# Last node stage of a four-layer graph network: TensorE turns the rows of a block two blocks, instead of one, before it multiplies them

## The chip, the cores and the metric

One Trainium2 chip, one of its cores. The metric is the device time of one execution in microseconds. The kernel has four layers; the change is in the second half of the last one.

## The reference

Four graph layers run one after the other on 50,000 nodes with 160 features (64 scalars and 32 vectors of three) and 25,000 edges. Each layer computes, cut to what matters here:

```python
agg = segment_sum(edge_feat, edge_dst)            # edge stage: messages summed per target node
# node stage of the last layer (L3), for every node:
s_s = xs * node_attr @ Ws_sc_a + xs * node_crystal_attr @ Ws_sc_c     # 64 scalars, two groups of weights
s_v = same with the 32 vectors and Wv_sc_a, Wv_sc_c
out = C_S * concat(s_s, s_v) + C_X * o            # o: made from agg
x   = _layernorm(x + out)                         # over the 160 features
```

So the node stage reads each node's row x and its aggregate row, adds the two, adds two products of x with small matrices, each scaled by one of the node's two gates, and normalises the row.

## The kernel before

Each layer l (0 to 3) has an edge stage, which writes the aggregates to memory, and then a node stage. A node stage goes over `NBLK` = 100 blocks b of 512 nodes; a block lies as 128 partitions with `BT` = 4 rows of 160 features each (`xn[:, k]`, 640 columns). Eight slots, `NRING` = 8, k = b % 8, hold the blocks in flight. The engines' programs are written out by hand, one instruction stream for each, with semaphores between them; on every engine the order is fixed, and a wait holds up all that stands behind it. In the last layer (l = 3, `G` = 2 groups of weights) the streams are, for step b:

- SyncE's queue, `node_loads`: wait for `stored[k]`, that is until the result of block b - 8 has left the slot; then load x of block b (line 476), and then the aggregates of block b + 2 (line 465).
- TensorE, `node_products`: the turn of block b (line 816: five 128x128 transposes, written T(b) below), once x of block b is in (`x_in`) and the PSUM pair `two_banks[b % 2]` is free, that is once ScalarE has copied turn b - 2 (`nturned_out`). Then the products of block b - 1 (line 846: eight fp32 matmuls that the trace shows as sixteen records, P(b-1) below). P(b) waits for the copy of turn b, for VectorE to be done with the first half of P(b-1) (`y_stt`; PSUM banks 4 and 5), and in its middle for ScalarE to be done with the second half (`second_gated`; banks 6 and 7).
- ScalarE, `node_copies`: issue the store of block b - 5 (line 959, from `STORE_LAG` = 5); copy turn b from PSUM to `nT[b % 2]` (line 963), once T(b) and P(b-2) are done; scale the second half of the products of block b - 1 into `second` (line 974, four instructions), once P(b-1) is done; the square root for block b - 3 (line 980); the normalisation of block b - 4 (line 986, four instructions).
- VectorE, `node_vectors`: add the first half of P(b), scaled, to the rows (line 1300, four instructions); then the statistics of block b - 1 (lines 1317 and 1328), and between them the reciprocal and the shift for block b - 2 (lines 1277 and 1282), which wait for ScalarE's square root.
- GpSimd, `add_both`: add the aggregates of block b to x once T(b) has read it (line 645), then the two scaled halves of block b - 1 (lines 651 and 654).

`steps` writes the first eight steps out, runs steps 8 to 95 as a loop with eight steps in its body, and writes the last ones out. `back(k, turn, lag, ring)` gives the slot and the turn of an earlier block, and `within(q, lo, hi)` says whether step q has work of that kind. The program waits that matter:

```python
wait(pe, nturned_out, node_count(l, b - 2))          # line 813, ahead of T(b)
wait(act, sc_ready, 2 * (b + (l * NBLK - 1)))        # line 962, ahead of the copy of turn b
act.wait_ge(sc_ready, 2 * (b + l * NBLK))            # line 970, ahead of the scaling of block b - 1
wait(sp, stored[k], node_slot(l, k, turn - 1) * 16)  # line 474, ahead of the load of x
```

Of the kernel before, what the change touches and what calls it, by code (L numbers as in the profile page):

```python
# [24 lines left out]
NBLK = 100  # L25
# [8 lines left out]
APPLY_LAG = [4, 3, 3, 4]  # L34
STORE_LAG = [5, 4, 4, 5]
A_LEAD = 2
NRING = 8
XGR = 4
AW = 2 + F
# [101 lines left out]
def back(k, turn, lag, ring=RING):  # L141

    return (k - lag) % ring, turn + (k - lag) // ring


def steps(eng, first, last, steady, body, ring=RING):

    lo, hi = steady
    for q in range(first, lo):
        body(q, q % ring, q // ring)  # L150
    with eng.Fori(0, (hi - lo) // ring) as i:
        for k in range(ring):
            body(i * ring + (lo + k), k, i + lo // ring)
    for q in range(hi, last):
        body(q, q % ring, q // ring)


def within(q, lo, hi):

    return lo <= q < hi if isinstance(q, int) else True  # L160


def wait(eng, sem, value):

    if isinstance(value, int) and value <= 0:
        return
    eng.wait_ge(sem, value)


def alone(eng, passed):  # L170

    eng.sem_inc(passed, 1)


def build(nc, nodes, front, back_rows, gate_rows, pairs, eattr, main, small, self_rows, mark_rows, out):
# [3 lines left out]
    with ctx:  # L179
        def sb(name, shape, dt=f32):  # L180
            return ctx.enter_context(nc.sbuf_tensor(name, shape, dt))

        def sem(name):
            return ctx.enter_context(nc.semaphore(name))
# [44 lines left out]

        arena = sb("arena", [P, NRING * BT * (F + AW)])  # L230
        o1, o2, o3, o4 = 512, 512 + 4 * 384, 512 + 4 * 384 + 4 * F, 1536 + 4 * 384 + 4 * F
# [4 lines left out]
        tot = arena[:, o4:o4 + TRING * 2 * (2 + AW3)].rearrange("p (r t c) -> p r t c", r=TRING, t=2)  # L236
        n1 = NRING * BT * F
        n2 = n1 + NRING * BT * AW
        xn = arena[:, 0:n1].rearrange("p (r c) -> p r c", r=NRING)
        an = arena[:, n1:n2].rearrange("p (r t c) -> p r t c", r=NRING, t=BT)  # L240
        second = same_all[:, 0:XGR * BT * F].rearrange("p (r t c) -> p r t c", r=XGR, t=BT)
        attr = sb("attr", [P, NRING, BT, 3])
        stats = sb("stats", [P, 2, BT, 6])
# [88 lines left out]
        nturned, nturned_out, sc_ready = sem("nturned"), sem("nturned_out"), sem("sc_ready")  # L332
# [6 lines left out]
        gated, second_gated, second_added = sem("gated"), sem("second_gated"), sem("second_added")  # L339
# [7 lines left out]
        NODE_STEADY = (NRING, 96)  # L347
# [13 lines left out]
        def node_count(l, b):  # L361
            return b + (l * NBLK + 1)
# [3 lines left out]
        def node_slot(l, k, turn):  # L366

            return turn + (l * node_uses[k] + 1)
# [18 lines left out]
        def _(sp):  # L387
# [26 lines left out]
            for l in range(4):  # L414
# [43 lines left out]
                def aggregate_load(b, k):  # L458
                    at = b if isinstance(b, int) else sp.snap(b)
                    if l in (0, 3):  # L460
                        wait(sp, x_added, b + ({0: 1, 3: NBLK + 1}[l] - NRING) if not isinstance(b, int) or b >= NRING else 0)
                    elif not isinstance(b, int) or b >= NRING:
                        wait(sp, sc_ready, 2 * (b + (l * NBLK + 1 - NRING)))
                    alone(sp, passed["sp"])
                    sp.dma_start(an[:, k].rearrange("p t c -> p (t c)"),
                                 arows[bass.ds(at, 1)].rearrange("o p c -> (o p) c")).then_inc(a_in[k], 16)

                def node_loads(b, k, turn):
                    if isinstance(b, int) and b == 0:
                        for n in range(A_LEAD):  # L470
                            aggregate_load(n, n)
# [4 lines left out]
                    sp.dma_start(xn[:, k], xrows[bass.ds(at, 1)].rearrange("o p c -> (o p) c")).then_inc(x_in[k], 16)  # L476
                    if within(b, 0, NBLK - A_LEAD):
                        aggregate_load(b + A_LEAD, (k + A_LEAD) % NRING)

# [190 lines left out]
        def _(pe):  # L670
# [26 lines left out]
            for j in range(4):  # L697
                a, b = (384, 448) if j < 2 else (448, 480)
# [7 lines left out]
            for l in range(4):  # L706
# [98 lines left out]

                def node_products(b, k, turn):

                    kk, tt = back(k, turn, 1, NRING)
                    has_new, has_old = within(b, 0, NBLK), within(b, 1, NBLK + 1)
                    if has_new:  # L810
                        to = two_banks[k % 2]
                        pe.wait_ge(x_in[k], node_slot(l, k, turn) * 16)
                        wait(pe, nturned_out, node_count(l, b - 2))
                        alone(pe, passed["pe"])
                        for c in range(5):
                            last = nc.tensor.transpose(to[:, c * P:(c + 1) * P], xn[:, k, c * CH:(c + 1) * CH], ident[:, :])  # L816
                        last.then_inc(nturned, 1)
                    if not has_old:
                        return
                    pe.wait_ge(nturned_out, node_count(l, b - 1))  # L820
                    base = 2 * (b + l * NBLK)
                    turned_x = [nT[:, kk % 2, c * P:(c + 1) * P] for c in range(5)]
                    mm = nc.tensor.matmul
                    if G == 1:
                        A, B = bank[4 + 2 * (kk % 2)], bank[5 + 2 * (kk % 2)]
                        wait(pe, y_stt, base - 4)
                        alone(pe, passed["pe"])
                        fresh = l == 0
                        if not fresh:
                            pe.wait_ge(a_in[kk], node_slot(l, kk, tt) * 16)  # L830
                            alone(pe, passed["pe"])
                            mm(A[:, 0:3 * F].rearrange("p (t c) -> p t c", t=3), ident[:, :], an[:, kk, 0:3, 2:AW], start=True, stop=False)
                        for c in range(4):
                            o, e = c * CH, min((c + 1) * CH, 3 * F)
                            last = mm(A[:, o:e], turned_x[c], sc[l][:, o:e], start=fresh, stop=fresh or c == 3)  # L835
                        last.then_inc(sc_ready, 1)
                        if not fresh:
                            mm(B[:, 0:F], ident[:, :], an[:, kk, 3, 2:AW], start=True, stop=False)
                        mm(B[:, 0:F], turned_x[4], sc[l][:, 3 * F + S:4 * F + S], start=fresh, stop=False)
                        mm(B[:, 0:S], turned_x[3], sc[l][:, 3 * F:3 * F + S], start=False, stop=True).then_inc(sc_ready, 1)  # L840
                    else:
                        two = lambda ap, n: ap.rearrange("p (g c) -> p g c", c=n)
                        W = two(sc[l], SCC)

                        def product(j, lo, hi, c, at, **flags):
                            return mm(two(bank[4 + j][:, 0:2 * F], F)[:, :, lo:hi], turned_x[c], W[:, :, at:at + hi - lo], **flags)  # L846
                        whole = dict(start=True, stop=True)
                        wait(pe, y_stt, base - 2)
                        alone(pe, passed["pe"])
                        product(0, 0, 128, 0, 0, **whole)  # L850
                        product(0, 128, 160, 1, 128, **whole)
                        product(1, 0, 96, 1, 160, **whole)
                        product(1, 96, 160, 2, 256, **whole).then_inc(sc_ready, 1)
                        wait(pe, second_gated, b - 1)
                        alone(pe, passed["pe"])
                        product(2, 0, 64, 2, 320, **whole)
                        product(2, 64, 160, 3, 384, **whole)
                        product(3, 0, 160, 4, 544, start=True, stop=False)
                        product(3, 0, 64, 3, 480, start=False, stop=True).then_inc(sc_ready, 1)

                steps(pe, 0, NBLK + 1, NODE_STEADY, node_products, NRING)

                pe.wait_ge(y_stt, 2 * NBLK * (l + 1))

# [555 lines left out]
```

## Time and profile before

| what | value |
|---|---|
| median of three runs | 4107.62 us (4105.41 to 4110.64) |
| profiled execution, its own time | 4101.09 us |
| span of the profiled execution | 4098.9 us |
| mean granted TensorE clock over the span | 0.949 |
| busy share of the span: TensorE, VectorE, ScalarE, GpSimd | 86%, 68%, 55%, 61% |
| last node stage: first turn of TensorE, last copy of turned rows on ScalarE | 3644.50 us, 4081.6 us |

The busy shares are means over stages with different limits. A span lies inside the execution's own time, and 2.2 us are outside it. Line numbers with L are those of the kernel. In the trace PE is TensorE's matmuls, PEld its weight loads, DVE VectorE, ACT ScalarE, POOL GpSimd; ACTq and SPq are instructions of the sequencers, the issues of transfers among them. An idle time is put down to what came last by the profile, which need not be what the program waited for.

### The profile page before, as it was taken

The numbers are of one execution on the slowest core, as the hardware profiler recorded it, in microseconds if no ns is written. First come the engines' busy times: TensorE is split into PE (matmuls) and PEld (weight loads), VectorE is DVE, ScalarE is ACT, GpSimd is POOL, SyncE is SP. The second block draws the span as 40 slices with busy tenths as digits, with TensorE's granted clock in tenths as the row PEclk, the third lists the DMA queues.
The fourth block names the chain that finished last, engine by engine and source line by source line (L and its number), as shares of the span: only waits on it lengthen the run. The fifth ranks groups of instructions, "written<-read, shape, count | busy, mean of one in ns | idle before, by whom it ended". The sixth has DMA issues, their size and how long they took to land.

```text
span 4098.9 us, 104392 instructions
## 1 busy us (share of the span) xinstructions
PE 3520.8 (86%) x26652; PEld 3264.2 (80%) x26652; DVE 2803.2 (68%) x10450; ACT 2255.1 (55%) x6189; POOL 2500.3 (61%) x3168
## 2 busy tenths in 40 slices
PE   0599998666659999989979999989989999977776
PEld 0599997656649999977769999977779999976665
DVE  0477775888876666668876666678866666656666
ACT  0244443555544444457765555567766666658888
POOL 0377776777766777756657777600036666657776
PEclk9999999777769999999999999999999999989999
DMA  9522222556642222259862222178842222136665
GB/s 390 179 82 63 61 56 86 187 196 200 202 137 59 58 57 55 48 192 300 298 200 64 62 61 57 39 271 300 298 130 56 54 52 50 44 109 223 222 226 193
DMA packets 423009, 575.44 MB, mean 140 GB/s; under 512 B 218250, under 2 KB 241802, under 8 KB 419144
## 3 DMA queue, kind: packets, MB, share of 16 engines
q1 hardware_dynamic: 280746, 293.10, 24.3%
q10 hardware_dynamic: 60512, 166.57, 10.3%
q0 software_dynamic: 81648, 114.57, 9.8%
q8 instruction: 43, 0.70, 0.1%
q14 instruction: 60, 0.49, 0.0%
HBM read 359.42 MB, written 233.39 MB: 145 GB/s over the span
## 4 chain that ended last, share of the span: by engine, by line
PE 60%; ACT 15%; POOL 8%; issue 8%; ACTq 3%; DMA 2%; DVE 2%; another core or an unknown queue 2%; POOLq 1%; SPq 1%; DVEq 0%
PE bank L734 17%; PE bank L767 12%; ACT arena L986 9%; PE bank L777 5%; PE bank L787 3%; PE bank L724 3%; PE bank L790 3%; PE bank L741 3%; PE bank L782 3%; POOL arena L632 3%; ACT same_all L974 3%; PE bank L759 3%; ACTq L959 2%; POOL arena L636 2%; ACT nT L963 2%
## 5 line engine op out<-in xcount | busy, mean ns | idle before, releaser
L545 POOL DMA_INDIRECT aggregates<-arena,meta x784 | 792.0, 1010 | 436.5 <-issue 252.5
L986 ACT ACTIVATE arena<-arena,shift,rstd 128x160 f32<-128x160 f32 x1600 | 699.3, 514 | 180.3 <-DVE shift L1251 177.6
L734 PE MATMUL bank<-same_all,msg 128*98 (+1 forms) x6272 | 750.7, 273 | 0.0
L533 POOL DMA_INDIRECT xg<-x_after,meta x588 | 584.7, 994 | 252.7 <-issue 249.7
L734 PEld LDWEIGHTS bank<-same_all,msg 128*98 128x98 f32 x6272 | 708.0, 165 | 0.1
L903 ACT ACTIVATE w<-bank 1x162 f32<-1x162 f32 (+1 forms) x784 | 257.9, 329 | 738.2 <-PE bank L767 736.5
L767 PE MATMUL bank<-w,arena 98*128 98x32 f32 (+1 forms) x4704 | 626.8, 270 | 0.0
L835 PEld LDWEIGHTS bank<-sc_cols,nT 128*128 128x128 f32 x2400 | 358.8, 220 | 288.7 <-issue 287.3
L767 PEld LDWEIGHTS bank<-w,arena 98*128 98x128 f32 x4704 | 588.6, 192 | 0.0
L835 PE MATMUL bank<-sc_cols,nT 128*128 128x128 f32 (+1 forms) x2400 | 371.3, 306 | 178.0 <-ACT nT L963 157.6
L1317 DVE BATCH_NORM_STATS2 stats<-arena 128x6 f32<-128x160 f32 x1600 | 455.5, 314 | 42.2 <-DVE arena L1310 5.8
L963 ACT ACTIVATE nT<-bank 128x640 f32<-128x640 f32 x400 | 281.6, 705 | 331.0 <-PE bank L835 165.0
L1206 DVE TENSOR_TENSOR arena<-bank,yv 128x192 f32<-128x192 f32 x294 | 105.2, 358 | 468.3 <-PE bank L787 284.5
L846 PE MATMUL bank<-sc_cols,nT 128*128 128x128 f32 (+4 forms) x1600 | 278.1, 328 | 106.7 <-ACT nT L963 64.8
L816 PE MATMUL bank<-ident,arena 128*128 128x128 f32 x2000 | 322.5, 298 | 47.7 <-DMA arena<-x_after 35.5
L846 PEld LDWEIGHTS bank<-sc_cols,nT 128*128 128x128 f32 x1600 | 241.0, 193 | 147.9 <-issue 126.9
L1310 DVE SCALAR_TENSOR_TENSOR arena<-bank,attr,arena 128x160 f32<-128x160 f32 x800 | 264.3, 379 | 66.0 <-PE bank L835 46.4
L816 PEld LDWEIGHTS bank<-ident,arena 128*128 128x128 f32 x2000 | 265.4, 165 | 50.1 <-issue 50.0
L1164 DVE COPY arena<-bank 98x512 f32<-98x512 f32 x392 | 269.2, 687 | 43.0 <-PE bank L734 27.7
L891 ACT ACTIVATE arena<-bank 98x512 f32<-98x512 f32 x392 | 231.9, 592 | 74.5 <-PE bank L734 74.4
L777 PE MATMUL bank<-weights,nT 128*128 128x128 f32 (+1 forms) x1764 | 256.3, 282 | 3.7 <-DVE msg L1231 3.7
L896 ACT ACTIVATE arena<-bank 128x128 f32<-128x128 f32 (+1 forms) x392 | 129.7, 331 | 232.4 <-PE bank L741 230.3
(153 smaller groups left out, 7359.5 us busy)
## 6 DMA issues: line engine op xcount, KB each, us to landing
arena<-aggregates SPq DMA_DIRECT2D x400, 324.0 KB, 4.0
x_after<-arena ACTq DMA_DIRECT2D x300, 320.0 KB
arena<-x_after SPq DMA_DIRECT2D x300, 320.0 KB
aggregates<-same_all ACTq DMA_DIRECT2D x4, 8100.0 KB, 72.3
arena<-nodes SPq DMA_DIRECT2D x100, 320.0 KB
out<-arena ACTq DMA_DIRECT2D x100, 320.0 KB
same_all<-sorted_dst SPq DMA_DIRECT2D x7, 1792.0 KB, 6.6
aggregates<-arena,meta POOLq DMA_INDIRECT x784, 2.3
```

The costliest lines, as they stand in the source:

```text
L533: gp.indirect_dma_start(xg[:, k % XGR, 4 + t * F:4 + (t + 1) * F], None, xtab[l], at).then_inc(gathered[k], 16)
L545: gp.indirect_dma_start(agg, at, tot[:, kk % TRING, t, 0:AW], None, bounds_check=NP - 1, oob_is_err=False).then_inc(spread[kk], 16)
L734: last = nc.tensor.matmul(bank[5 + t][0:MR, c * P:(c + 1) * P], msg[:, k2, t, c, :], same_all[:, bass.ds(here[t], P)], start=True, stop=True)
L767: last = nc.tensor.matmul(to, aggT[:, t, (d + 1) * P:(d + 2) * P], of, start=True, stop=True)
L777: last = nc.tensor.matmul(bank[3][:, a:e], xT[:, k2, c * P:(c + 1) * P], w1[l][:, a:e], start=True, stop=True)
L816: last = nc.tensor.transpose(to[:, c * P:(c + 1) * P], xn[:, k, c * CH:(c + 1) * CH], ident[:, :])
L835: last = mm(A[:, o:e], turned_x[c], sc[l][:, o:e], start=fresh, stop=fresh or c == 3)
L846: return mm(two(bank[4 + j][:, 0:2 * F], F)[:, :, lo:hi], turned_x[c], W[:, :, at:at + hi - lo], **flags)
L963: nc.scalar.activation(nT[:, k % 2, :], two_banks[k % 2][:, 0:5 * P], ACT.Copy).then_inc(nturned_out, 1)
L986: last = nc.scalar.activation(row, row, ACT.Identity, bias=shift[:, kk, t:t + 1], scale=rstd[:, kk, t:t + 1])
L1164: nc.vector.tensor_copy(aggT[:, 0, :], bank[5][0:MR, :]).then_inc(summed_out[0], 1)
L1317: last = nc.vector.bn_stats(stats[:, ks % 2, j, :], xn[:, ks, j * F:(j + 1) * F])
```

## The change

In layer 3 alone TensorE multiplies in step b the rows turned in step b - 2, not those turned in step b - 1. Its stream becomes T(b), P(b-2), T(b+1), P(b-1), and has one step more. All other engines' streams, the buffers and the numbers of instructions stay as they are.

```diff
+TURN_LEAD = [1, 1, 1, 2]
...
-                    kk, tt = back(k, turn, 1, NRING)
-                    has_new, has_old = within(b, 0, NBLK), within(b, 1, NBLK + 1)
+                    late = TURN_LEAD[l]
+                    kk, tt = back(k, turn, late, NRING)
+                    has_new, has_old = within(b, 0, NBLK), within(b, late, NBLK + late)
...
-                    pe.wait_ge(nturned_out, node_count(l, b - 1))
-                    base = 2 * (b + l * NBLK)
+                    pe.wait_ge(nturned_out, node_count(l, b - late))
+                    base = 2 * (b + (l * NBLK + 1 - late))
...
-                        wait(pe, second_gated, b - 1)
+                        wait(pe, second_gated, b - late)
...
-                steps(pe, 0, NBLK + 1, NODE_STEADY, node_products, NRING)
+                steps(pe, 0, NBLK + TURN_LEAD[l], NODE_STEADY, node_products, NRING)
```

## Rows read from the trace of the kernel before

**Rows 1.** The chain that ended last, 3690 to 4080 us, its shares.

```profile
by line: ACT arena L986 35.4%; ACT same_all L974 26.2%; issue 17.2%; ACTq L959 9.0%; ACT std L980 4.1%; PE bank L846 2.1%; ACT nT L963 1.2%; ACTq L961 0.9%; ACTq L970 0.8%; ACTq L172 0.7%; DVE arena L1300 0.5%; ACTq L167 0.4%; ACTq L969 0.4
```

**Rows 2.** Timeline, ScalarE: start, us, instructions, idle before and its releaser.

```profile
3799.94 0.70 ACT L963 ACTIVATE nT<-bank 128x640 f32<-128x640 f32 x1 [0.76 <-PE bank L816]
3800.54 1.25 ACT L974 ACTIVATE same_all<-bank,attr 128x160 f32<-128x160 f32 x4
3801.84 1.76 ACT L986 ACTIVATE arena<-arena,shift,rstd 128x160 f32<-128x160 f32 x4
3803.82 0.34 ACTq L959 DMA_DIRECT2D out<-arena  x1
3804.34 0.70 ACT L963 ACTIVATE nT<-bank 128x640 f32<-128x640 f32 x1 [0.75 <-PE bank L816]
3804.95 1.24 ACT L974 ACTIVATE same_all<-bank,attr 128x160 f32<-128x160 f32 x4
```

**Rows 3.** Timeline of the same stretch, TensorE and VectorE.

```profile
3799.06 0.71 PE L816 MATMUL bank<-ident,arena 128*128 128x128 f32 x5
...
3800.88 2.75 PE L846 MATMUL bank<-sc_cols,nT 128*128 128x256 f32 x16 [1.12 <-ACT nT L963]
...
3803.47 0.71 PE L816 MATMUL bank<-ident,arena 128*128 128x128 f32 x5
...
3803.78 1.26 DVE L1300 SCALAR_TENSOR_TENSOR arena<-bank,attr,arena 128x160 f32<-128x160 f32 x4
```

**Rows 4.** Who waited for whom, 3672 to 4070 us: us in total, times, longest.

```profile
ACT nT L963 <- PE bank L816: 59.9, 80, 0.8
PE bank L846 <- DVE arena L1300: 38.8, 33, 1.4
```

**Rows 5.** Timeline of the first blocks of the stage, TensorE, VectorE and ScalarE.

```profile
3647.27 4.45 PE L846 MATMUL bank<-sc_cols,nT 128*128 128x256 f32 x16
...
3651.56 0.71 PE L816 MATMUL bank<-ident,arena 128*128 128x128 f32 x5
...
3652.10 2.68 PE L846 MATMUL bank<-sc_cols,nT 128*128 128x256 f32 x16
...
3653.51 1.26 DVE L1300 SCALAR_TENSOR_TENSOR arena<-bank,attr,arena 128x160 f32<-128x160 f32 x4 [2.38 <-PE bank L846]
...
3654.89 1.25 ACT L974 ACTIVATE same_all<-bank,attr 128x160 f32<-128x160 f32 x4 [1.21 <-issue]
```

**Rows 6.** Timeline, stores on ScalarE's sequencer and the loads of x behind them.

```profile
3664.69 0.34 ACTq L959 DMA_DIRECT2D out<-arena  x1
...
3667.13 0.35 SPq L476 DMA_DIRECT2D arena<-x_after  x1
...
3795.01 0.34 ACTq L959 DMA_DIRECT2D out<-arena  x1
...
3797.61 0.33 SPq L476 DMA_DIRECT2D arena<-x_after  x1
...
3825.91 0.34 ACTq L959 DMA_DIRECT2D out<-arena  x1
...
3829.74 0.33 SPq L476 DMA_DIRECT2D arena<-x_after  x1
```

**Rows 7.** Timeline, a load of x and the turn of the same block.

```profile
3712.10 0.33 SPq L476 DMA_DIRECT2D arena<-x_after  x1
...
3715.22 0.71 PE L816 MATMUL bank<-ident,arena 128*128 128x128 f32 x5
```

**Rows 8.** Transfers, 3690 to 4080 us: queue 1 is SyncE's; KB, median us to landing.

```profile
q1 hardware_dynamic: 24891, 56.98, 48.6%
...
arena<-aggregates SPq DMA_DIRECT2D x85, 324.0 KB, 4.4
```

**Rows 9.** Busy us (instructions) by stretch, then granted clock, DMA share, GB/s.

```profile
700.00:1230.00 530.00, 329.62 (x1747) 303.89 (x1746) 429.67 (x1818) 266.94 (x653) 386.53 (x750) 0.71 0.55 184
...
3950.00:4050.00 100.00, 74.62 (x475) 65.27 (x476) 68.50 (x316) 83.27 (x229) 71.74 (x79) 1.00 0.70 226
```

## The prediction

> **What bounds the kernel now.** I read first the chain that ended last, over the steady part of the stage. Nearly all of it is ScalarE: its normalisation, its scaling of the second half, its root, its issues; TensorE has 2.1% of it [rows 1]. Then one period of ScalarE's timeline: copy of the turned rows at 3799.94, scaling at 3800.54, normalisation from 3801.84, store issued at 3803.82, next copy at 3804.34, next scaling at 3804.95 [rows 2]. From scaling to scaling it is 4.41 us, and nothing in it stands still except around the store's issue. The trace puts 0.76 us of idle time ahead of each copy down to TensorE's turn [rows 2], 59.9 us in 80 waits [rows 4]. That is not what the copy waits for. Counted from the stage's start, the copy at 3799.94 is that of block 35, and the turn at 3799.06 [rows 3] is T(36); T(35) was over a block earlier. The idle time is the store's issue, 0.34 us, and the instructions around it.
>
> TensorE keeps up with room: P(35) starts at 3800.88, right after the copy of turn 35; T(37) follows at 3803.47 [rows 3]; ScalarE takes up P(35) at 3804.95. So the stage costs 4.41 us a block because ScalarE's own work is that long. A different order on TensorE can't shorten this; it can only lengthen it.
>
> **The change part by part.** It adds and removes no instruction: 100 turns and 100 products either way. What moves is T(b+2): from behind P(b) to ahead of it. No transfer is issued by TensorE, so none moves with it, and SyncE's and GpSimd's queues keep their order. Three things follow.
>
> *The copy's wait.* The copy of turn b now finds its turn done two blocks earlier than it asks for. Price: nothing, since it does not wait today.
>
> *P(b) behind T(b+2).* T(b+2) needs the PSUM pair that the copy of turn b frees, so after that copy come turn and product, not the product alone. At full clock T starts at 3651.56, P at 3652.10, and ScalarE's scaling of it at 3654.89 [rows 5]: 3.33 us from the start of a turn to the scaling of the product behind it. If T(37) started where P(35) does today, at 3800.88, P(35) would be ready for ScalarE at 3804.21, 0.74 us ahead of 3804.95. With x in place the added 0.54 us ahead of P is thus hidden by ScalarE's normalisation; without that cover it would be up to 0.54 us a block. VectorE starts on P's first half 1.41 us after P's start [rows 5]. At the latest P that ScalarE tolerates (2.79 us before the scaling) that is 3803.57, and today it starts at 3803.78 [rows 3]; hidden, with 0.2 us to spare.
>
> *T(b+2) needs x of block b + 2 earlier.* This is where the cost is. To hold ScalarE's pace T(37) must start by 3804.95 - 3.33 = 3801.62, where today it starts at 3803.47: 1.85 us earlier. Is x there by then? The load of x waits for the slot's old result to be stored, and it is late already. Load and turn of block 17 are 3.12 us apart [rows 7]; 1.85 us off that leaves 1.27 us between the load's issue and the latest good turn, and no load is that quick. TensorE would wait for x with P(b) queued behind the wait, though everything that P(b) needs is there, and ScalarE waits for P(b). What is late next is the store, and through it the load three blocks on. So the stage gets a loop of its own, through three blocks:
>
> - Store issued to load of the slot's next x issued: alone 2.44 us; the eight pairs from 3795.01 to 3829.74 have a mean of 3.8, the first 2.60 and the last 3.83 [rows 6], the five between 3803.82 and 3825.47 have 4.2. I take 4.0. Ends 3.2 and 4.4.
> - Load issued to turn started: the trace has no landing for x. Above: the aggregates' load, issued 0.67 us behind it on the same queue, lands after 4.4 us, so 5.07 after x's issue, and each load takes 1.10 us of the engines (48.6% of 390 us over 172 loads) [rows 8]: x at 3.97 at the latest. Below: where a store shares the engines, the aggregates' part takes up to twice that, x lands at 2.87; block 17 shows that 3.12 can be enough [rows 7]. I take the middle, 3.4, and 0.1 for the wait's end: 3.5. Ends 3.0 and 4.1.
> - Turn started to scaling started: 3.33 [rows 5].
> - Scaling started to next store issued: 3803.82 - 3800.54 = 3.28 [rows 2].
>
> Sum 4.0 + 3.5 + 3.33 + 3.28 = 14.1 us for three blocks, 4.70 a block, where ScalarE alone gives 3 x 4.41 = 13.23. That is 0.29 us a block. It holds for the blocks whose slot must be emptied first, from block 8 on, and the spare time of the first ones is used up by about block 12: 88 blocks, +26 us. With the low ends the loop is 12.8 us and costs nothing; with the high ends 15.1, 5.04 a block, +55.
>
> The Trainium skill (DMA: Bandwidth & Descriptors, "Anatomy of one DMA") fits a transfer as about 2.0 us plus its bytes over 436 GB/s, for GpSimd's path; for 320 KB that is about 2.75 us. The lone store agrees (2.44 us with SyncE's reaction), the crowded ones don't. By the page both transfers would take 2.75 us and the loop would be 12.4 us, below 13.23: no loss. This stage isn't the page's lone transfer, so I stay with the rows.
>
> *Ends.* At the start, on the half clock, P(0) has T(2) ahead of it: one turn, 1.3 us, and a wait for its x, so +2 us. At the end P(98) has no turn ahead: -0.5. Together about +1.
>
> Total +27 us: 4101.1 + 27 = 4128 us for an execution like the profiled one. The median of the runs is 6.5 us above that one, so the median becomes about 4135 us.
>
> **The rivals.**
>
> *No change* (x comes in time). Price as above: if store to load and load to turn together stay below 13.23 - 6.61 = 6.62 us, ScalarE remains the bound. For it: alone, the store's part is 2.44; transfers spread out once the pace slackens. The page's rule is part of this. Against it: the crowded pairs alone take 4.2 of the 6.62. 4100 to 4114 us, chance 0.16.
>
> *Faster.* If the 59.9 us that ScalarE is said to wait for turns [rows 4] were a true wait, turns made a block earlier would remove it: about 4048 us. It decides if a copy starts on its own block's turn. Against it is the count of blocks above, and the chain, which has hardly any TensorE. Chance 0.04.
>
> *Slower, and the clock falls too.* At the half clock P(0) took 4.45 us against 2.68 [rows 5]. The first layer's node stage, with TensorE busy 62% of the time, had a granted clock of 0.71; this stage, at 75%, has 1.00 [rows 9]. After the change it would be about 70%. If the clock fell in a third of the blocks, each would add some 2.3 us to a loop of three: about +23 us more, 4158 us. Chance 0.10.
>
> *VectorE becomes the bound:* it already has TensorE waiting 38.8 us [rows 4], and only 0.2 us are spare. A P later than that makes y late, but P is then late anyway; it is inside the forecast.
>
> **How the numbers follow.** Forecast, x late with the clock up: 0.70, 4115 to 4165, likeliest 4135. With the clock rival at 0.10, slower is 0.80; no change 0.16; faster 0.04. Within 0.2%, 8 us, a measurement of this kernel tells nothing from no change. For 8 in 10 the range must take in part of the no-change case and leave the dearest of the clock's: 4107 to 4163 us.
>
> **What would show it.** TensorE's turn (line 816) gets waits for the load of x, on most blocks from the tenth on; ScalarE's scaling (line 974) gets true waits for the products, some 0.3 us a block, uneven from block to block; the chain goes through the load, TensorE and the store. ScalarE's own pieces keep their lengths. The idle time ahead of the copy stays near 0.75 us, though it may be put down to something else. Wrong would be: a copy that starts sooner after the store; turns that don't wait for x; or transfers so much quicker at a slacker pace that the period stays 4.41.

## The result, and the profile after

| | before | changed |
|---|---|---|
| median of the runs | 4106.51 us (4 runs, 4103.34 to 4110.64) | 4157.29 us (4 runs, 4150.96 to 4159.69) |
| ratio to before | | 1.0121, 95% interval 1.0103 to 1.0138 |
| span of the profiled execution | 4098.9 us | 4157.5 us |
| last node stage, first to last copy of turned rows | 3645.84 to 4081.6, 435.8 us | 3658.55 to 4140.1, 481.5 us |
| mean over its 99 steps | 4.40 us | 4.86 us |

The kernel is 50 us slower, and 46 us of that lie in the stage that was changed. The two profiled executions are 58.6 us apart; the rest arose ahead of the stage, which begins 12.7 us later, in code that is the same in both. Line numbers of the changed kernel are higher by one for SyncE's loads (466 and 477) and by two from TensorE's turn on: turn 818, products 848, store 961, copy 965, scaling 976, root 982, normalisation 988.

Who waited for whom, from 3680 to 4130 us of the changed kernel (us in total, times, longest), which answers to [rows 4]:

```profile
PE bank L818 <- DMA arena<-x_after: 92.9, 50, 3.3
ACT same_all L976 <- PE bank L848: 43.1, 23, 4.8
PE bank L818 <- ACT nT L965: 38.4, 31, 1.7
ACT nT L965 <- PE bank L848: 37.4, 50, 0.8
...
ACT nT L965 <- ACT arena L988: 24.6, 33, 0.8
...
ACT nT L965 <- PE bank L818: 6.1, 8, 0.8
```

TensorE now waits for x ahead of its turn in half of the blocks, 1.9 us each. ScalarE's wait for the products, which the stage hardly had, is 43.1 us in 23 waits, and this is nearly all of the stage's loss. The idle time ahead of the copy is there as before, 0.75 us a block, 68 us in 91 waits, but most of it is now put down to the products and to the normalisation instead of the turn. It never was a wait for the turn; turns made two blocks ahead left it alone.

The chain that ended last, 3690 to 4130 us, for comparison with [rows 1]:

```profile
by line: ACT arena L988 19.3%; DMA out<-arena 17.9%; DMA arena<-x_after 14.7%; PE bank L848 14.2%; ACT same_all L976 14.0%; issue 8.8%; PE bank L818 3.6%; ACTq L961 3.3%; ACT std L982 2.2%; ACTq L173 0.4%; ACT nT L965 0.4%; ACTq L963 0.3%; 
```

Store, load of x, turn and products have half of it, where ScalarE's own work had nearly all. Landing times from 3680 to 4130 us (KB, median us to landing), beside [rows 8]. The count is that of the issues; the trace has a landing for only 12 of these loads of x, 11 of the aggregates and 22 of the stores:

```profile
arena<-x_after SPq DMA_DIRECT2D x92, 320.0 KB, 3.0
arena<-aggregates SPq DMA_DIRECT2D x90, 324.0 KB, 3.4
out<-arena ACTq DMA_DIRECT2D x91, 320.0 KB, 3.8
```

And busy time, granted clock, DMA share and GB/s, beside [rows 9]:

```profile
3680.00:4130.00 450.00, 318.68 (x1929) 283.30 (x1928) 276.99 (x1284) 338.86 (x917) 290.69 (x321) 0.95 0.60 200
```

The granted clock of the steady stretch was 1.00 and is now 0.95. The timeline shows how one loss comes about, from a load's issue to the scaling:

```profile
3747.95 0.34 ACTq L961 DMA_DIRECT2D out<-arena  x1
...
3752.17 0.33 SPq L477 DMA_DIRECT2D arena<-x_after  x1
...
3752.89 0.71 ACT L965 ACTIVATE nT<-bank 128x640 f32<-128x640 f32 x1 [0.75 <-PE bank L848]
3753.49 1.25 ACT L976 ACTIVATE same_all<-bank,attr 128x160 f32<-128x160 f32 x4
3755.96 0.73 PE L818 MATMUL bank<-ident,arena 128*128 128x128 f32 x5 [3.25 <-DMA arena<-x_after]
3756.53 4.34 PE L848 MATMUL bank<-sc_cols,nT 128*128 128x256 f32 x16
...
3757.31 0.71 ACT L965 ACTIVATE nT<-bank 128x640 f32<-128x640 f32 x1 [0.75 <-PE bank L818]
...
3760.99 1.25 ACT L976 ACTIVATE same_all<-bank,attr 128x160 f32<-128x160 f32 x4 [2.98 <-PE bank L848]
```

A store issued at 3747.95 lets its slot's next x go out only at 3752.17. TensorE stands still for 3.25 us and turns at 3755.96. The products behind it take 4.34 us, where 2.68 is their length at full clock: the clock has gone to its lower level after the wait. ScalarE, done with its copy at 3758.02, gets them at 3760.99.

### The profile page after: what moved, and what is told of

Same layout as the page of the kernel before. It is cut to its first block, busy times and chain, and to the rows that moved or that the text cites. A ratio compares the mean times of both kernels' runs of the same rounds, so it can differ in the third digit from the quotient of the medians.

```text
span 4157.5 us, 104381 instructions
## 1 busy us (share of the span) xinstructions
PE 3546.9 (85%) x26652; PEld 3290.7 (79%) x26652; DVE 2800.9 (67%) x10450; ACT 2265.4 (54%) x6189; POOL 2499.6 (60%) x3168
## 4 chain that ended last, share of the span: by engine, by line
PE 64%; ACT 10%; POOL 8%; issue 6%; DMA 6%; ACTq 2%; DVE 2%; another core or an unknown queue 1%; POOLq 1%; SPq 1%; DVEq 0%
PE bank L735 17%; PE bank L768 12%; ACT arena L988 6%; PE bank L778 5%; PE bank L725 3%; PE bank L788 3%; PE bank L791 3%; PE bank L742 3%; PE bank L783 3%; POOL arena L633 3%; PE bank L834 3%; PE bank L760 2%; PE bank L837 2%; DMA arena<-x_after 2%; PE bank L848 2%
## 5 line engine op out<-in xcount | busy, mean ns | idle before, releaser
L837 PEld LDWEIGHTS bank<-sc_cols,nT 128*128 128x128 f32 x2400 | 359.9, 221 | 287.3 <-issue 286.2
L848 PE MATMUL bank<-sc_cols,nT 128*128 128x128 f32 (+4 forms) x1600 | 290.4, 339 | 4.1 <-ACT nT L965 2.5
L848 PEld LDWEIGHTS bank<-sc_cols,nT 128*128 128x128 f32 x1600 | 257.8, 204 | 28.5 <-issue 8.0
L725 PE MATMUL bank<-ident,xg 128*128 128x128 f32 x1176 | 206.9, 286 | 59.5 <-DMA xg<-x_after,meta 49.0
```

The lines of the kernel that those rows point to most:

```text
L725: last = nc.tensor.transpose(bank[0][:, c * P:(c + 1) * P], xg[:, k % XGR, 4 + c * CH:4 + (c + 1) * CH], ident[:, :])
```

## The experiments

The lengths of the stage are from the first to the last copy of turned rows. The kernel before, run beside each batch on the same chip, took 4105 us in the batch of the small filler and the shorter store, and 4896 to 4955 us in the other three, where the edge stages are slower and repeat worse. The changed kernel's last node stage is alike in both (481.5 us at a span of 4157.5, and 485.8 at 4960.7), so the stage's length in the trace is the sharper measure. The kernel before has a trace only from where it takes 4105 us (435.8 us). Each ratio is against the kernel before of its own batch.

**The changed kernel once more**

> The changed kernel itself once more, beside the others, so that they share a chip. Ratio to before 1.010 to 1.014 if the whole takes 4100 us there; on a chip whose edge stages are slower the same 40 to 60 us are a smaller share, 1.008 to 1.012.

Measured: 1.0067 (1.0034 to 1.0100) in a batch with slow edge stages; the stage took 485.8 us, granted clock 0.93. The ratio is below the 1.008 to 1.012 expected for such a place, and its interval only overlaps it. By the medians the loss is 43 us; by the stage, set against the 435.8 us of the kernel before, it is 50.

**The store taken out of the loop.** Lead two; the normalised rows go to a buffer of their own, and the load of x waits for the normalisation of the slot's old block, not for its store. The store's own wait moves to ScalarE, which normalises into the buffer once the store of eight blocks earlier has left it.

```diff
-                    wait(sp, stored[k], node_slot(l, k, turn - 1) * 16)
+                    if l == 3 and (not isinstance(b, int) or b >= NRING):
+                        sp.wait_ge(normed, node_count(l, b - NRING))
...
-                            last = nc.scalar.activation(row, row, ACT.Identity,
+                            to_row = done_rows[:, kk, t * F:(t + 1) * F] if l == 3 else row
+                            last = nc.scalar.activation(to_row, row, ACT.Identity,
```

> Lead two, but the normalised rows go to a buffer of their own, so the load of x waits for the normalisation of block b - 8 and not for its store. Loop theory (x is late because its slot is stored first): 3.5 us of store leave a loop of 14.1 us over three blocks, 10.6 is far below 13.23, so ScalarE is the bound again: 4107 us, 4100 to 4115. Rival one (the turn ahead of the products is itself the cost, by the PSUM pair or by 0.54 us ahead of P): it stays above 4140. Rival two (TensorE's clock fell and that is the cost by itself): between the two, unless the clock rises with the waits gone.

Measured: 0.9996 (0.9971 to 1.0020), stage 441.1 us. Waits of this kernel, 4510 to 4920 us, by its own lines: turn at line 822, copy 970, scaling 981, products 852:

```profile
PE bank L822 <- ACT nT L970: 106.3, 88, 1.5
...
ACT same_all L981 <- PE bank L852: 2.6, 1, 2.6
```

The order on TensorE is that of the changed kernel. TensorE waits for the copy before each turn, 1.2 us a block, as that order demands, and ScalarE pays for it nowhere but in one wait of 2.6 us. The granted clock of the stretch is 1.00 again. So neither the turn ahead of the products nor the PSUM pair is the cost; the late x is the cause, of the clock's fall too. The same kernel in another batch:

> The changed kernel with the rows in a buffer of their own, once more, for a ratio on another chip. Loop theory: 0.998 to 1.002 of before. Rival (the lead costs by itself): 1.005 or more.

Measured: 1.0006 (0.9978 to 1.0034), stage 439.8 us.

**Control: the separate buffer with lead one**

> Control: the same separate buffer with lead one. Loop theory: nothing waits for x before, so the same time as before, 4100 to 4115 us; one more wait on ScalarE per block may cost up to 0.05 us each, 5 us. Should it be faster than before, x was late there too.

Measured: 1.0013 (0.9993 to 1.0033), stage 439.3 us. As expected: with lead one no x is waited for, so taking the store away gains nothing. The stage is even 3.5 us longer than in the trace of before, and this kernel, not that one, is what lead two with the buffer has to be set against.

**The store one block later, lead one.** Meant to close the same loop over three blocks without touching TensorE's order:

```diff
-STORE_LAG = [5, 4, 4, 5]
+STORE_LAG = [5, 4, 4, 6]
```

> Lead one as before, but the last layer's store is issued one block later (lag six instead of five). TensorE's order is that of before. Loop theory: the loop through store, load, turn, products and ScalarE now closes over three blocks instead of four, as with lead two, with the same 14.1 us: 4130 to 4175 us, near the changed kernel. Rival (the order on TensorE is the cost): as before, plus one block's drain, 4107 to 4115 us.

Measured: 0.9921 (0.9897 to 0.9945), stage 388.1 us, 3.92 a step. The expectation failed outright, and for a reason to which the profile of before had the key. ScalarE of this kernel:

```profile
4642.70 0.96 ACT L974 ACTIVATE same_all<-bank,attr 128x160 f32<-128x160 f32 x3 [0.84 <-PE bank L846]
4643.47 0.34 ACTq L959 DMA_DIRECT2D out<-arena  x1
...
4644.01 1.75 ACT L986 ACTIVATE arena<-arena,shift,rstd 128x160 f32<-128x160 f32 x4
4645.66 0.70 ACT L963 ACTIVATE nT<-bank 128x640 f32<-128x640 f32 x1
```

At lag five the store of a block is issued right behind its normalisation: the sequencer waits for the end of it, and ScalarE stands still for 0.75 us before its copy [rows 2]. At lag six the rows are long ready, the store is issued while the scaling runs, and the copy follows the normalisation without a gap. That gain hid the loop, and it changed the loop too: the store now goes out 0.5 us after a scaling starts in the mean (0.9 at most), not 3.28. With the forecast's other terms that is 4.0 + 3.5 + 3.33 + 0.5 = 11.3 us for three blocks, 3.78 a block, and the loop does show in the waits (4510 to 4860 us):

```profile
PE bank L816 <- DMA arena<-x_after: 42.1, 49, 1.6
ACT same_all L974 <- PE bank L846: 24.1, 49, 1.1
```

TensorE waits for x here with lead one as well. That the measured 3.92 a block is near 3.78 was worked out afterwards and is no test by itself.

**The store one block later, lead two**

> Lead two and the store one block later. Loop theory: the loop closes over two blocks, 12.8 to 14.1 us for two, 6.4 to 7.05 a block against 4.41: 90 blocks, +180 to +240 us, 4290 to 4350 us. Rival (the order alone costs): like the changed kernel, about 4157 us.

Measured: 1.0221 (1.0196 to 1.0247), +98 us by the medians; the first copy is at 4498.48, the last at 5032.4, a stage of 534.0 us, 5.39 a step. Above the rival, far below the expected 6.4 to 7.05, which had the store at 3.28 us behind the scaling as before. With the early store the forecast's loop is 11.3 us over two blocks, 5.67, near the measured 5.39. In this trace the store's part is 3.2 us in the mean where 4.0 was forecast, the load's 3.1 instead of 3.5, and from turn to scaling it is 3.9 instead of 3.33, at a lower granted clock. Against the kernel above it, the lead costs 146 us of stage instead of 46: one block less costs more where the loop already is the limit, and the clock's fall is in it too. Waits, 4560 to 5010 us, where the granted clock is 0.89:

```profile
ACT same_all L976 <- PE bank L848: 149.0, 66, 5.8
PE bank L818 <- DMA arena<-x_after: 137.4, 75, 4.5
```

**TensorE kept active while it waits for x.** Two matmuls more per block in the last layer of the changed kernel, ahead of the wait for x, which moves behind them:

```diff
+                            for _ in range(2):
+                                nc.tensor.matmul(to[:, 0:512], ident[:, :], sc[l][:, 0:512], start=True, stop=True)
+                            pe.wait_ge(x_in[k], node_slot(l, k, turn) * 16)
```

> The changed kernel with two more matmuls of 128x512 per block on TensorE (about 1 us), between the wait for the PSUM pair and the wait for x, their result overwritten by the turn. They fill time in which TensorE waits for x, and keep it active. Clock theory (part of the loss is the clock that falls after the waits): granted clock in the stage 0.99 to 1.00 instead of 0.95, and 10 to 25 us less than the changed kernel. Rival (the transfers' loop is all of it): the clock rises or not, the time stays, or grows by up to 20 us where x was there and the filler stood in its way.

Measured: 1.0109 (1.0073 to 1.0146), granted clock 1.00, stage 492.6 us. Inconclusive: the filler took 1.95 us in the timeline, not 1 us, and made TensorE the bound. Its busy time, first after the length of the stretch, is 437.04 of 440 us:

```profile
4470.00:4910.00 440.00, 437.04 (x2224) 318.84 (x2222) 269.48 (x1245) 334.58 (x889) 283.34 (x311) 1.00 0.60 199
```

Small waits of ScalarE in nearly every block (38.4 us in 88) took the place of the few large ones. With half the filler:

> The changed kernel with one more matmul of 128x512 per block (0.65 us) ahead of the wait for x, in place of the two that took 1.3 us. From the copy of a turn to the scaling of its products it is then 0.24 + 0.65 + 3.33 = 4.22 us; ScalarE leaves 4.31, so it should hide where x is there. Clock theory (about half of the changed kernel's loss is the clock that falls after long waits for x): granted clock 0.99 to 1.00 in the stage, products never over 2.9 us, stage 445 to 460 us from first to last copy of a turn against 471 to 473. Rival (all of it is the transfers): the clock rises, the stage stays at 465 to 475.

Measured: 1.0087 (1.0070 to 1.0104), +36 us where the changed kernel has +50; stage 470.6 us. The 445 to 460 us expected were not reached, and as it was written down the rival (465 to 475) is what came. But the expectation set both against 471 to 473 us, a figure for the changed kernel that lacked its first blocks; the right one is 481.5, so the stage is 11 us shorter, which the rival does not give. Its waits and its clock, 3680 to 4100 us:

```profile
ACT same_all L981 <- PE bank L853: 25.7, 23, 3.3
```

```profile
3680.00:4100.00 420.00, 368.72 (x2024) 283.87 (x2023) 266.55 (x1232) 327.21 (x880) 280.20 (x308) 1.00 0.63 205
```

and one of its losses on TensorE:

```profile
3870.81 0.76 PE L823 MATMUL bank<-ident,arena 128*128 128x128 f32 x5 [1.28 <-DMA arena<-x_after]
3871.41 2.68 PE L853 MATMUL bank<-sc_cols,nT 128*128 128x256 f32 x16
3873.93 1.02 PE L820 MATMUL bank<-sc_cols,ident 128*128 128x512 f32 x2
```

x is still late, but the products behind the wait take 2.68 us. ScalarE's waits for products fall from 43.1 to 25.7 us. So more TensorE work gave less time. The filler takes 1.02 to 1.10 us, not the 0.65 of the expectation, and what it costs by itself was not measured apart, so by this reading the 11 us are what the clock gave back less that cost. The transfers were not quicker: from a store's issue to the issue of the slot's next load it is 3.77 us in the mean, against 3.56 in the changed kernel, and from a load to a turn that waited for it 3.57 against 3.43.

**A shorter store.** Lead two, only two of the four rows stored:

```diff
-                        act.dma_start(orows[bass.ds(done, 1)]..., xn[:, kk])
+                        n_out = 2 * F if l == 3 else 4 * F
+                        act.dma_start(orows[bass.ds(done, 1), :, 0:n_out]..., xn[:, kk, 0:n_out])
```

> The changed kernel, but the last layer stores only two of the four rows of a partition: half of the output stays unwritten. Store to load shrinks from 3.6 us to about 2.5 to 3.0, and the loads behind it have less beside them. Loop theory: most waits of ScalarE for the products go, 435 to 450 us from first to last copy of a turn, ratio to before 0.999 to 1.004. Rival (the time from load to turn alone, or the order, is the cost): the stage stays above 460 us.

Measured: 1.0040 (1.0026 to 1.0054), stage 453.3 us, just beyond the expected 450. Landing times, and the wait of ScalarE for the products, 3680 to 4080 us:

```profile
arena<-x_after SPq DMA_DIRECT2D x87, 320.0 KB, 2.9
out<-arena ACTq DMA_DIRECT2D x86, 160.0 KB, 3.5
```

```profile
ACT same_all L977 <- PE bank L848: 15.2, 17, 2.5
```

From a store's issue to the issue of the slot's next load it is now 3.09 us in the mean instead of 3.56, from the load to a turn that waited for it 3.31 instead of 3.43. Two thirds of ScalarE's waits were gone, and the granted clock fell in five blocks after the first ones instead of eleven. The stage stands at the edge of ScalarE's pace, where tenths of a microsecond count.

**Both limits taken away.** Lead one, store one block later and the separate buffer; and the same with lead two.

> Lead one, store one block later and the rows in a buffer of their own: ScalarE no longer stands still around the store's issue, and no load waits for a store. If ScalarE's own work is then the bound, the period is 4.41 - 0.75 = 3.66 us, 75 us less than before in the stage; if the store's loop was no limit at lag six, 3.89 as there, 50 us less.

Measured: 0.9864 (0.9806 to 0.9921), stage 381.1 us, 3.85 a step.

> The same with lead two. From the copy of a turn to the scaling of its products it is 0.24 + 3.33 = 3.57 us, just below 3.66: loop theory says that the lead then costs 0 to 10 us against lead one, and nothing of the 50 us. Rival (the lead costs by itself, whatever the transfers do): 40 us or more against lead one.

Measured: 0.9867 (0.9824 to 0.9910), stage 380.0 us. With no store in the loop the lead costs nothing, and gains nothing. The version with lead one once more:

> Lead one, store a block later, rows in a buffer of their own, once more, for a ratio on another chip: the stage was 55 us shorter than before in its trace, so 0.985 to 0.989 where the whole takes about 4100 us.

Measured: 0.9890 (0.9861 to 0.9918), stage 380.9 us. This version and its twin with lead two are the fastest of the study, 53 to 54 us below the kernel before by the medians. They were run only in batches with slow edge stages. Waits of the lead-one version, 4490 to 4830 us:

```profile
PE bank L850 <- DVE arena L1309: 46.6, 65, 1.1
...
ACT same_all L979 <- PE bank L850: 20.2, 44, 0.7
```

No transfer is among them. What keeps it above the expected 3.66 us is, by these waits, ScalarE's wait for the products (20.2 us, 0.2 a block), and TensorE in turn waits for VectorE in most blocks. No run took VectorE's part away.

## Why the prediction was right, and where its sizes were off

*ScalarE is the bound, and the trace's wait for the turn is none.* Right: an idle time put down to turns stayed when the turns came earlier, and went when the store came a block later. I had priced it as the store's issue "and the instructions around it" and looked no further; it was the wait for the block's own normalisation ahead of that issue, and taking it away gained 50 us, as much as this change lost.

*P(b) behind T(b+2) is hidden.* Right, shown by lead two with the separate buffer: 441.1 and 439.8 us against 439.3.

*x is late, and a loop through store, load, turn and products sets the pace.* Right as a mechanism, though x was waited for in half of the blocks and not in most. With the store out of the loop the loss is gone; with half the store about a third of it is left; with one block less in the loop it triples.

*The loop's size.* Forecast +27 us, measured +50. The terms, read from the changed kernel's trace as means: from a store's issue to the issue of the slot's next load 3.56 us where I had 4.0, from a load to a turn that waited for it 3.43 (3.5), from turn to scaling 3.37 at full clock (3.33), from scaling to the next store 3.30 (3.28). With them the averaged loop is 13.7 us, 4.55 a block, and the change would cost only about +14 us. What failed is the step from an averaged loop to a pace. Where the loop is shorter than 3 x 4.41, ScalarE gains nothing back; where it is longer, ScalarE loses the excess. The loss came in 23 waits of up to 4.8 us, with blocks at ScalarE's usual 4.42 between them. Terms near the limit have to be summed as excesses, not as means.

*The clock.* Here the forecast failed as it stood: it had x late "with the clock up", and the clock did not stay up. The 4157 us measured are those of the rival in which x is late and the clock falls too (4158 us, chance 0.10), 22 us above the likeliest value. Of the 22 waits of ScalarE for products after the first blocks, there are 11 in which the turn and the products ran partly or wholly at the lower clock, and those waited 30.7 us; the other 11 waited 9.8. From turn to scaling it is 3.37 us at full clock in these waits, and 4.96 to 6.33 in those with the fall. Taking off what the lower clock added, at most the wait itself, leaves 10.4 of the 30.7. So about 20 us of the 40 are the late x and 20 the clock, by this count of one trace. Without the clock's part some 26 of the stage's 46 us are left, near the forecast's 27. That agreement is luck: the transfers were taken too long and the loss at the limit too small, and the two made up for each other. The rival's 23 us for the clock came out by luck too: it had a third of the blocks, each adding 2.3 us to a loop of three, where the trace has 11 blocks at 1.8 us each. That the clock has a part is borne out by the filler, not its exact size: +36 instead of +50 us.

*The transfers.* The median store took 3.8 us to its landing and the median load of x 3.0. The fit of the Trainium skill (DMA: Bandwidth & Descriptors, "Anatomy of one DMA"), which the page gives for GpSimd's path, makes an estimate of 2.75 us for each. In this stage the store lies well above that and the load a little.

## What to carry to other kernels

Before an engine's work is pushed ahead, ask what the earlier work reads, and count through how many blocks the chain from a slot's store to its next load, through all engines, comes back to itself: one block less there can cost more than the move hides. Close to the limit, judge such a chain by its late cases, since the engine at the bound never earns back what they take. And look for an issue or a wait right behind the work that it depends on, in the stream of the engine that is the bound: here one more block of lag on the store gained as much as the order of TensorE lost.

## What the runs showed that was not expected

- TensorE's clock fell in a stage with an average busy share of 71% (318.68 of 450 us), to its level of 1.2 GHz, in eleven blocks after waits of 1.96 to 3.3 us for x. It did not fall after every such wait: there were 19 of that length, and after eight of them the products kept their 2.68 us, after one of 3.21 us too. In the kernel with the small filler, whose waits for x ahead of the turn were 1.6 us at most, it fell once. At the lower level, wholly or in part, the products took 3.8 to 5.1 us.
- A transfer issued by ScalarE's sequencer costs ScalarE 0.75 us a block if its rows have just been written, and nothing that shows if they were written a block earlier.
- The edge stages' time depends on where or when the kernel runs: the kernel before took 4105 us in some batches and 4896 to 4955 us in others. In the two traces of the changed kernel, 4157.5 and 4960.7 us long, the four node stages, each from its first to its last copy of turned rows, together differ by 8 us, so nearly all of the difference lies outside them. What makes it was not looked into.
